# Exponentials, transposes and casts of a cross-attention unit in two pieces of 4096 keys instead of four of 2048

## What is computed

```
q = _fq_sym(q, axis=-1)                       # rounded to integers times a step, per query
k = _fq_sym(k, axis=-1)
v = _fq_sym(v, axis=2)
attn = jnp.einsum('bhqd,bhkd->bhqk', q, k)
attn = jax.nn.softmax(attn.astype(jnp.float32), axis=-1)
attn = _fq_unsigned(attn, axis=-1)            # 0..255 times (row maximum / 255)
out = jnp.einsum('bhqk,bhkd->bhqd', attn, v)
```

## Time and profile before

| | us |
|---|---|
| median of 3 runs (lowest, highest) | 6527.99 (6514.9, 6553.14) |
| the profiled execution, its device time | 6548.42 |
| the profiled execution, its span | 6546.9 |
| window 500 to 5220 of it, which lies wholly in the changed stage | 4720.0 |

### The profile page before, as it was taken

One profiled execution on the slowest core, in us unless ns is written; L12 is line 12 of the kernel. 1 busy time (PEld: TensorE's weight loads), 2 busy tenths in 40 slices (PEclk: granted clock), 3 DMA queues, 4 the chain that ended last, 5 costly groups with the idle time before them and its releaser, 6 DMA issues. The chain is left out here.

```text
span 6546.9 us, 142949 instructions
## 1 busy us (share of the span) xinstructions
PE 4634.3 (71%) x49686; PEld 2154.8 (33%) x49686; DVE 5643.9 (86%) x7682; ACT 4741.1 (72%) x6485; POOL 4506.7 (69%) x3196
## 2 busy tenths in 40 slices
PE   6736666667766666666676666666666646769999
PEld 3412222222222222222222222222222233454555
DVE  7579999999999999999999999999999955872222
ACT  3329999999898898888898899999899843331111
POOL 1238888888888898888888888888898833420000
PEclk9769999999999999999999999999999978979999
DMA  3138777777777777777777777777777730010000
GB/s 119 51 73 143 139 144 143 142 140 143 141 143 137 138 147 137 136 143 140 138 138 143 140 140 142 146 139 143 139 140 143 141 99 4 0 35 3 6 6 10
DMA packets 2231970, 735.70 MB, mean 112 GB/s; under 512 B 2175779, under 2 KB 2209412, under 8 KB 2225573
## 3 DMA queue, kind: packets, MB, share of 16 engines
q1 hardware_dynamic: 2196261, 576.08, 43.4%
q0 software_dynamic: 35456, 157.33, 13.9%
HBM read 168.97 MB, written 27.26 MB: 30 GB/s over the span
## 5 line engine op out<-in xcount | busy, mean ns | idle before, releaser
L804 DVE TENSOR_SCALAR_CACHE_REDUCE scores<-ring,step 128x2048 f32<-128x2048 f32 (+2 forms) x2560 | 4782.2, 1920 | 70.4 <-PE ring L731 58.0
L863 ACT ACTIVATE n_op<-scores,bias 128x2048 uint8<-128x2048 f32 x2048 | 4076.2, 1997 | 285.5 <-DVE m_rest L811 285.4
L679 POOL CAST nT<-pairs 128x2048 f16<-128x2048 uint8 x2048 | 3791.4, 1890 | 532.5 <-DMA pairs<-n_op 513.3
L731 PE MATMUL ring<-x_all,q_op 128*128 128x512 bf16 x8192 | 2225.4, 385 | 676.5 <-DVE scores L804 585.7
L731 PEld LDWEIGHTS ring<-x_all,q_op 128*128 128x128 bf16 x8192 | 682.7, 98 | 1881.7 <-DVE scores L804 1180.0
L728 PE MATMUL ring<-x_all,q_op 128*128 128x512 bf16 x2048 | 633.0, 391 | 725.3 <-DVE scores L804 709.0
L743 PE MATMUL pO<-nT,v_op 128*32 128x128 f16 x32768 | 662.0, 224 | 157.0 <-ACT att_g L881 111.2
L743 PEld LDWEIGHTS pO<-nT,v_op 128*32 128x32 f16 x32768 | 484.3, 98 | 607.5 <-issue 512.1
L728 PEld LDWEIGHTS ring<-x_all,q_op 128*128 128x128 bf16 x2048 | 116.8, 97 | 997.8 <-DVE scores L804 979.3
L863 ACT ACTIVATION_READ_ACCUMULATOR n_op<-scores,bias 128x1 f32 x2048 | 396.0, 193 | 0.0
L1642 DVE TENSOR_TENSOR h_up<-h_gate,pUp 128x512 f32<-128x512 f32 x112 | 77.0, 687 | 298.1 <-ACT h_gate L1631 298.1
(11 more groups left out here) (195 smaller groups left out, 3553.0 us busy)
## 6 DMA issues: line engine op xcount, KB each, us to landing
x_all<-keys_transposed POOLq DMA_DIRECT2D x128, 768.0 KB, 8.6
v_st<-value_integers POOLq DMA_DIRECT2D x128, 256.0 KB, 3.5
pairs<-n_op SPq DMA_TRANSPOSE x2048, 2.8
keys_transposed<-kT_s POOLq DMA_DIRECT2D x32, 384.0 KB, 3.5
x_all<-in_x SPq DMA_DIRECT2D x2, 4096.0 KB, 14.9
cT<-in_ctx_T SPq DMA_DIRECT2D x32, 256.0 KB, 3.0
q_op<-queries_transposed POOLq DMA_DIRECT2D x384, 16.0 KB, 8.4
value_integers<-v_int SPq DMA_DIRECT2D x1, 4096.0 KB, 12.2
```

Of the source, the lines that this page charges most:

```text
L679: nc.gpsimd.tensor_copy(nT[par][:, j * EK:(j + 1) * EK, :].rearrange("p (a c) b -> p a c b", c=2), src).then_inc(s_un, 1)
L731: mm = nc.tensor.matmul(slot(t, j)[:, n * BANK:(n + 1) * BANK], q_op[b][:, t * P:(t + 1) * P], k_op[b][:, at + n * BANK:at + (n + 1) * BAN ...
L804: nc.vector.tensor_scalar(score[t % 2][:, at:at + width * BANK], slot(t, j)[:, 0:width * BANK], step[b][:, t:t + 1], None, ALU.mult, ALU.m ...
L863: nc.scalar.activation(n_op[par][:, j * EW:(j + 1) * EW], score[par][:, j * EW:(j + 1) * EW], ACT.Exp, bias=bias[par][:], scale=-1.0, accu ...
```

## The change

`NE` becomes 2, so a piece is 4096 keys: two exponentials, two transposes and two casts for each unit, and two sums. The ACT order becomes DEN E0 FIN OC E1, and in POOL's order the load of keys stands behind the first piece of 4096, the rest as before.

```
-        NE = 4
+        NE = 2
...
-        ACT_STEPS = "DEN E0 FIN E1 OC E2 E3".split()
+        ACT_STEPS = "DEN E0 FIN OC E1".split()
...
                         unpack(u, t, 0)
                         if t == 3 and exists(u + 2 * TG):
                             keys(g + (h + 2) // H, (h + 2) % H, i + 2)
-                        unpack(u, t, 1)
                         if t == 3 and h == 0 and exists(u - H * TG):
                             store(g - 1)
-                        unpack(u, t, 2)
-                        unpack(u, t, 3)
+                        unpack(u, t, 1)
                         if t == 1 and (not isinstance(i, int) or 2 <= i + 1 < HEADS):
                             values(i + 1, (h + 1) % 2, (h + 1) % H, exists(u + 3 * TG))
```

## The result

The changed kernel takes 6870.4 us (median of 4 runs, 6849.3 to 6890.9) against 6521.4 us (4 runs, 6502.5 to 6553.1) of the kernel before on the same chip: a ratio of 1.053, 95% interval 1.049 to 1.057. It is slower, as forecast, but by 349 us and not by 140, and outside the range of 6597 to 6770. The profiled execution took 6875.9 us with a span of 6874.3.

A forecast was written before the change was run, and what follows sets the result against it. The prediction took DVE to set the pace, with FIN to D0 a chain on PE without room. Its terms, 177 - 40 + 3 = +140 us on the median of 6528, gave 6668 us, range 6597 to 6770.

The forecast's parts named there:

- the chain: From FIN on ACT through AV0, M4, AV1, N0 on PE to D0: a later FIN delays D0 equally.
- The term of +177 us: FIN at t = 2 comes 1.39 us later behind larger exponentials, in each of 127 heads.
- AV0, M4, AV1, N0 and D0 therefore come 1.39 us later: Step on PE and DVE behind FIN: its delay of 1.39 us passes on unchanged as far as D0.
- The term of -40 us for late keys: At the load of keys, t = 3's last transpose escapes the keys, recovering DVE waits; between 0 and -64 us.
- the room at t = 0: Casts behind the keys end at 3047.0, AV0 is due at 3050.4; at the longest landing 2.8 us of wait remain.
- The 54.1 us of DVE's waits: DVE's waits for PE and ACT today, taken as those in 4000 us of the stage.
- the 64 us: DVE's waits today put at some 64 us over 4720 us, the most the late-keys term could give back.
- The fixed time of an exponential: On ACT, 299 ns for each exponential, so one piece of 4096 keys takes 3.68 us.
- the 7270 us of that rival: Rival: t = 3's second transpose stays behind the keys and AV0 waits 4.7 us in each head; chance 0.06.
- no change: Rival: FIN's delay finds 1.4 us of cover on PE or DVE; about 6530 us, chance 0.06.
- faster: Rival: t = 3 no longer waits behind the load of keys, DVE gets 64 us back; 6467 us, chance 0.04.

The follow-up runs named there:

- e7: Kernel before, with one more unused copy of 128x768 on ACT just ahead of FIN; 6656.0 us, ratio 1.017.
- e5: Changed kernel, with two matmuls of M3 done twice in every unit, at t = 2 just ahead of the wait for FIN; 6745.0 us, ratio 1.033.
- e1: Changed kernel, with only ACT's order altered to DEN FIN E0 OC E1, so FIN precedes the first exponential; 6580.9 us, ratio 1.006.
- fourth experiment: Kernel before, with exponentials in two pieces of 4096 in ACT's new order, transposes and casts still in four of 2048; 6875.9 us, ratio 1.051.
- e2: Kernel before, with only ACT's order altered to DEN E0 E1 FIN OC E2 E3, so FIN follows two exponentials; 6942.4 us, ratio 1.060.
- e3: Kernel before, with transposes and casts in two pieces of 4096, exponentials still in four of 2048 in ACT's old order; 6595.8 us, ratio 1.006.

## Why the prediction was wrong

- **The bound and the chain were right.** DVE sets the pace, and FIN to D0 is a chain on PE without room. FIN comes 1.43 us later after OC (forecast 1.39), AV0 waits 2.29 us (forecast 2.2), D4 1.09 us (forecast 1.06), and heads at full clock are 38.7 us long (forecast 38.6). The term of +177 us stands, and e7 gives it again at half the size.
- **The step that failed is "AV0, M4, AV1, N0 and D0 therefore come 1.39 us later".** It took the durations of AV0, M4, AV1 and N0 behind the wait from a trace in which the clock was up, and with the longer wait the clock fell: FIN's end to D0 takes 4.88 us instead of 3.3 in 104 of 124 heads, so D0 comes some 3 us later in them and not 1.39. Over 124 heads the changed kernel has 72 + 2 x 33 = 138 stretches at half clock against 23 + 2 x 3 = 29 before; 109 x 1.6 = 174 us, which the sum lacked. With 177 that makes 351 us, against 349 measured. So close an agreement is partly luck: in the two traces the 124 heads take 5027.6 and 4694.7 us, 333 more, of which 124 x 1.41 = 175 are the delay and 158 all the rest, casts included. I had looked at the clock (0.99) as a state of the stage and not as something that the change could move. The run e5 shows it by itself: the same delay, and some 130 us less where the clock mostly stays up. Why it stayed up at the wait in 20 heads of the changed kernel is open.
- **The term of -40 us for late keys was too hopeful.** The last transpose of t = 3 did escape the keys, and t = 0 paid, both as described. Landing took 3.7 us (forecast 4.1), a cast 3.60 us (3.69), an exponential 3.71 us (3.68). But PE's waits for casts are 31.7 us in 4720, 31.2 before, so the term gave about nothing; the 8 waits would have been 2.3 us each for FIN anyway, so some 18 us of them are not added. Without FIN's lateness, in e1, the same casts cost 100 us of waits: in the median head AV0 of t = 0 begins 0.24 us behind the end of its last cast, which is the shortest distance in that trace, so no room is left. I had computed the room at t = 0 with the delay of FIN in it and took it for a property of the casts. Two readings behind the term were too large as well. The 54.1 us of DVE's waits were all there are in 4720 us, so the 64 us, and the low end of the range with them, were 10 us too far. And the late casts of t = 3 make only 24 of the 45.5 us for PE (DVE's waits at D4 of t = 1), not nearly all.
- **The fixed time of an exponential.** 299 ns from the earlier trace rows forecast 3.68 us and 3.70 were measured between starts. The Trainium skill's 93 ns (Perfetto Trace Analysis, section Optimizing Scalar/DVE Operations) would have given 3.89, as an estimate, so the rows of this kernel were the better source. That section also says that breaking up instructions that cause bubbles on other engines may let work complete sooner. The fourth experiment agrees: the unbroken exponentials alone give the ratio of 1.051. But e1 shows that moving FIN ahead of them does nearly as well.
- **The rivals.** The second transpose of t = 3 escapes the keys, so the 7270 us of that rival are out, as are no change and faster. The range of 6597 to 6770 had no case in which one delay sets off another.

## What to carry to other kernels

Where a small operation frees a buffer for the engine with the strictest order, ask what now stands ahead of it when its neighbours grow, and move it ahead of them: here one word in ACT's order was worth some 310 us. A new wait on TensorE is not only its own length; look at how long TensorE idles in it and price the work behind it at the lower clock too. Merging pieces saves fixed time on engines that are not the bound, and coarsens the only thing that mattered there, when a result is ready.

## What the runs showed of the hardware

TensorE's granted clock fell from 1.00 to 0.50 at waits of 0.9 to 2.8 us for FIN, in more heads the longer the wait was. Of 124 heads each:

| kernel | PE's wait for FIN, us | heads with a stretch at half clock at the wait | FIN's end to D0 without / with it, median us |
|---|---|---|---|
| before | 0.86 | 8 | 3.34 / 4.82 |
| e7, smaller delay | 1.59 | 33 | 3.31 / 4.84 |
| e5, two more matmuls ahead of the wait | 1.86 | 39 | 3.31 / 4.88 |
| changed | 2.29 | 104 | 3.31 / 4.88 |
| e4, large exponentials alone | 2.29 | 97 | 3.31 / 4.88 |
| e2, FIN late in the kernel before | 2.84 | 124 | none / 4.88 |

The Trainium skill, TensorE: Matmul & The Clock Gate, section HAM oscillation, describes a periodic wait for a DMA, of some 3 to 5 us, that throttles PE anew in each tile, so that the cost is paid once a tile and not once. The trace agrees that it is paid anew, 1.57 us in each such head; here shorter waits, and for ScalarE, were enough.

Five waits of DVE are left that have nothing to do with FIN. The profile gives them as 11.3 us for "issue" in the changed kernel and as 8.6 us for ACT in the kernel before. They stand at one place in both, the first copy for t = 1 in the heads 32, 48, 64, 80 and 96, counted from 0, where a new pass of the loop over groups begins. They are 2.2 to 2.5 us each in all kernels with casts of 4096 and 1.6 to 2.0 in those with casts of 2048. Why the casts change their length stays open.
